# Moving the fourth step size from chunk 1 to chunk 4 and re-spreading the layer-norm squares in a selective-scan kernel

## The chip, the cores and the metric

The kernel runs on one core of a Trainium2 chip. The metric is the device time of one execution in microseconds (us), median of three runs. The core has five engines with a program each: TensorE (PE, matmuls), VectorE (DVE), ScalarE (ACT), GpSimd (POOL) and SyncE (SP, which issues the DMAs). They are ordered against each other by semaphores alone: each engine runs its own list in order, and a waiting instruction holds up all behind it.

## The reference, cut to what matters

Input x is 16 batches of 1024 steps by 512 channels. Two layers follow, each on a layer norm of x and added to x:

```
xn = layernorm(x)                               # layer norm 1
xp = xn @ x_proj_w.T                            # 64 + 16 + 16 columns: d_rank, B, C
delta = softplus(d_rank @ dt_proj_w.T + dt_b)   # the step size, 512 channels
h[t] = exp(delta * A) * h[t-1] + delta * B * xn # 16 states per channel
y[t] = sum over the states of h[t] * C + xn * D
x = x + y
weights = layernorm(x) @ router_w + router_b    # layer norm 2
...                                             # the 127 highest rows of each batch go through
                                                # attention and an MLP; the others take layernorm(x)
```

The change lies in the first layer's phase, the scan phase; the router's weights are its last product.

## The kernel before, in words

The scan phase (`scan_phase`) takes the 16 batches one after the other. A batch has 16 chunks of 32 channels. A chunk has 4 groups, each of 4 states x 32 channels = 128 partitions, and a group's tile is 128x1024, all 1024 steps. So a batch has 64 tiles. (c,g) is group g of chunk c. Batch 0 and batch 15 are written out, the others run in a loop over pairs of batches.

For each tile: ACT makes `decay` = exp(A * delta) into one of two PSUM buffers (L600); DVE makes `inp` = dx * B (L722), in chunks 1 and 3 to 13 POOL does it for group 3 (L844, the table `OWN_AT`); DVE scans, `hid` (L733); POOL multiplies by C, `ch` (L879); PE sums the states into `ps_y` (`sum_states`, L399). After a chunk ACT copies the sum (`copy_y`, L615), PE turns it (`turn_y`, L408), and DVE adds it to x (`add_y`, L743). The addition for chunk c stands in DVE's list behind the third scan of chunk c+1, so it needs `ch` (c,3) by then. `hid`, `ch` and `inp` have four buffers each, one per group. ACT's list per chunk: `decay` for groups 2 and 3, `copy_y`, `copy_dx` (L608), `decay` for groups 0 and 1 of the next chunk; `beside` puts other work between them at four places, 0 ahead of group 2's decay, 1 behind `copy_dx`, 2 and 3 behind the two decays. At the top of the file tables say at which (chunk, place) on ACT, or (chunk, group) on PE and POOL, that other work stands:

- The step size of a block of 128 channels (k = 0 to 3, each used by four chunks): PE makes two halves of z into the one bank `aux` (`step_size`, L382), ACT reads each half twice (`z_half`, L509 and L510) and then runs four passes (`exp_log`, L517 to L524), and POOL makes four more steps (`delta`, L853, L856, L860, L865), placed by the table `DELTA`. Blocks 0 to 2 are made for the next batch in chunks 12, 13 and 15 (`Z`); block 3 for the current batch, in chunk `Z3`. Chunks 12 to 15 are its users.
- Layer norm 1 of the next batch (`SUMS1`) and layer norm 2 of the batch before (`SUMS2`): 17 steps each, 0 to 7 sums (L541), 8 the mean (L544), 9 to 16 squares (L547), then `rstd`, three small operations. POOL finishes them (`newton`, L805 to L828) at `FINISH1` = (7,0) and `FINISH2` = (2,1).
- `copy_rw` (L528) puts the router's weights into `aux` at (2,0); DVE's `router` (L755) reads it behind the scans of chunks 2 and 3.
- The rows of the next batch are normalised by ACT (L470), turned by PE into `aux` (`turn_xhat`, L365) and copied (L483) in chunks 7 to 10, and projected in chunks 10 and 11.

`aux` is one PSUM bank; its users take turns by `aux_emptied` and `aux_full`, and the router's use of it is guarded by `router_sum`.

Of the kernel before, what the change touches and what calls it, by code (L numbers as in the profile page):

```python
# [26 lines left out]
TC = L // P  # L27
# [9 lines left out]
PROJECT = (((10, 0), (10, 0), (10, 1), (10, 1)), ((10, 3), (11, 0), (11, 0), (11, 1)))  # L37
COPY_PROJ = ((10, 3), (11, 3))

SUMS1 = {(5, 1): range(0, 2), (5, 2): range(2, 4), (5, 3): range(4, 8), (6, 0): range(8, 10), (6, 1): range(10, 12), (6, 2): range(12, 14), (6, 3): range(14, 17)}  # L40
SUMS2 = {(0, 1): range(0, 2), (0, 2): range(2, 4), (0, 3): range(4, 8), (1, 0): range(8, 10), (1, 1): range(10, 12), (1, 2): range(12, 14), (1, 3): range(14, 17)}
MAKE_OUT = ((3, 1), (3, 1), (3, 2), (3, 2), (3, 3), (3, 3), (3, 3), (3, 3))
NORM1 = 7


Z = (12, 13, 15)
Z3 = 1


DELTA = {(13, 0): (1, 0, 0), (13, 1): (1, 0, 1), (13, 2): (1, 0, 2), (13, 3): (1, 0, 3),  # L50
# [3 lines left out]

RW_COPY = (2, 0)
ROUTER = (2, 3)
# [10 lines left out]
USE = {key: u for u, key in enumerate(USES)}  # L67
NUSE = len(USES)
# [8 lines left out]
def xhat_slot(k, par):  # L77

    return (0, k) if k < 2 else (1 + par, k - 2)


def scan_phase(nc, semaphores, x, A_log, w_xproj, w_dt, dt_b, D_col, router_w, router_b, ident_c, nsum_c, bc_dram,
               x1_dram, w_dram, out, nb_run=B):

    with ExitStack() as ctx:
# [83 lines left out]
        aux_emptied = sem("aux_emptied")  # L169
# [13 lines left out]
        router_sum = sem("router_sum")  # L183
# [18 lines left out]
        def has(b, least):  # L202

            return not isinstance(b, int) or b >= least
# [145 lines left out]
        @block.tensor  # L350
        def _(pe):
            def aux_free(b, key):

                u = USE[key]
                if has(b, 1) or u > 0:
                    pe.wait_ge(aux_emptied, b * NUSE + u)

            def turn_xhat(b, t):

                aux_free(b, ("xhat", t))  # L360
                if t == 0 and has(b, 2):
                    pe.wait_ge(router_sum, b * TC - TC)
                pe.wait_ge(xh_ready, b * TC + t + 1)
                for k in range(KD):
                    last = pe.transpose(aux[:, k * P:(k + 1) * P], xh[:, t % 2, k * P:(k + 1) * P], ident[:])  # L365
                last.then_inc(aux_full, 1)

            def project(b, par, h, ks=range(KD)):

                if 0 in ks:  # L370
                    aux_free(b, ("proj", h))
                for k in ks:
                    last = pe.matmul(aux[0:R + 2 * N, :], xproj[:, k, :],
                                     xhT[:, xhat_slot(k, par)[0], xhat_slot(k, par)[1], h * HALF:(h + 1) * HALF],
                                     start=(k == 0), stop=(k == KD - 1))
                if KD - 1 in ks:
                    last.then_inc(aux_full, 1)

            def step_size(b, k, h):

                aux_free(b, ("z", k, h))
                pe.matmul(aux[:], dtw[:, k * P:(k + 1) * P], xpT[0:R, h * HALF:(h + 1) * HALF],  # L382
                          start=True, stop=True).then_inc(aux_full, 1)

            def sum_states(b, par, c, g):

                if g == 0 and (has(b, 1) or c > 0):

                    pe.wait_ge(y_added, b * CHUNKS + c)
                k = c // NT  # L390
                if g == 0:
                    i, j = xhat_slot(k, par)
                    for q in range(4):
                        pe.matmul(ps_y[q * CH:(q + 1) * CH, 0:2 * P],  # L394
                                  dskip[:, k, c % NT * CH:(c % NT + 1) * CH],
                                  xhT[:, i, j, q * 2 * P:(q + 1) * 2 * P], start=True, stop=False)
                pe.wait_ge(ch_ready, tile(b, c, g) + 1)
                for q in range(4):
                    last = pe.matmul(ps_y[q * CH:(q + 1) * CH, 0:2 * P], nsum[:],  # L399
                                     ch[:, g, q * 2 * P:(q + 1) * 2 * P],  # L400
                                     start=False, stop=(g == GROUPS - 1))
                last.then_inc(ch_summed, 1)

            def turn_y(b, c):

                pe.wait_ge(ysb_ready, b * CHUNKS + c + 1)
                for t in range(2):
                    last = pe.transpose(ps_y[:, (2 + t) * P:(3 + t) * P], ysb[:, t * P:(t + 1) * P], ident[:])  # L408
                last.then_inc(yt_ready, 1)

            pe.wait_ge(consts_in, 16 * NCONST)
            for t in range(TC):
                turn_xhat(0, t)
            for h in range(2):
                project(0, 0, h)
            for k in range(3):
                for h in range(2):
                    step_size(0, k, h)
            pe.wait_ge(dskip_ready, KD)

            def body(b, par):
                final = is_last(b)
                for c in range(CHUNKS):
                    if c > 0:
                        turn_y(b, c - 1)
                    elif has(b, 1):
                        turn_y(b - 1, CHUNKS - 1)
                    for g in range(GROUPS):
                        sum_states(b, par, c, g)

                        for h, at in ((0, (-1, 3)), (1, (0, 0))):
                            if (c, g) == (Z3 + at[0], at[1]):
                                step_size(b, 3, h)
                            for k in range(3):
                                if (c, g) == (Z[k] + at[0], at[1]) and not final:
                                    step_size(b + 1, k, h)
                        if final:
                            continue
                        for t in range(TC):
                            if TURN[t] == (c, g):  # L440
                                turn_xhat(b + 1, t)
                        for h in range(2):
                            for k in range(KD):
                                if PROJECT[h][k] == (c, g):
                                    project(b + 1, 1 - par, h, (k,))

            batches(pe, body)
            turn_y(nb_run - 1, CHUNKS - 1)

            pe.wait_ge(wcol_ready, nb_run)  # L450
            pe.wait_ge(aux_emptied, nb_run * NUSE)
            pe.transpose(aux[0:nb_run * TC, 0:P], wcol[:, 0:nb_run * TC], ident[:]).then_inc(wt_ready, 1)
# [3 lines left out]
        def _(act):  # L456
# [66 lines left out]
                act.wait_ge(z_act, n + 4)  # L523
                nc.scalar.activation(tu[:], tu[:], ACT.Identity, scale=-1.0, bias=1.0).then_inc(z_act, 1)  # L524

            def copy_rw(b):

                nc.scalar.activation(aux[:], rw[:], ACT.Copy).then_inc(rw_ready, 1)  # L528

            def sums(b, par, steps, norm, m, chain_act):  # L530
# [114 lines left out]
            def beside(b, par, c, place):  # L645

                at = (c, place)
                if c == Z3 and place == 1:
                    z_half(b, 3, 0)
                if c == Z3 and place == 3:  # L650
                    z_half(b, 3, 1)
                    exp_log(b, 3)
                if has(b, 1):
                    if at == RW_COPY:
                        copy_rw(b - 1)
                    if at in SUMS2:
                        ln2_sums(b - 1, 1 - par, SUMS2[at])
                    for t in range(TC):
                        if MAKE_OUT[t] == at:
                            make_out(b - 1, 1 - par, t)  # L660
                if is_last(b):
                    return
                if at in SUMS1:
                    ln1_sums(b + 1, 1 - par, SUMS1[at])
                if at == (NORM1, 2):
                    for t in range(2):
                        normalise(b + 1, 1 - par, t)
                for t in range(TC):
                    if COPY_XHAT[t] == at:
                        copy_xhat(b + 1, 1 - par, t)  # L670
                        if t + 2 < TC:
                            normalise(b + 1, 1 - par, t + 2)
                for h in range(2):
                    if COPY_PROJ[h] == at:
                        copy_proj(b + 1, h)
                if c in Z and place == 1:
                    z_half(b + 1, Z.index(c), 0)
                if c in Z and place == 3:
                    z_half(b + 1, Z.index(c), 1)
                    exp_log(b + 1, Z.index(c))  # L680
# [20 lines left out]
            batches(act, body)  # L701
            last = nb_run - 1
            copy_y(last, CHUNKS - 1)
            copy_rw(last)
            ln2_sums(last, 1, range(17))
            for t in range(TC):
                make_out(last, 1, t)
# [1017 lines left out]
```

## Time and profile before

| | us |
|---|---|
| median of 3 runs | 4733.67 (4727.59 to 4733.85) |
| profiled execution | 4730.44 |
| its span | 4728.3 |
| DVE busy | 3868.9 (82%) |
| POOL busy | 3543.6 (75%) |
| PE busy | 2806.7 (59%) |
| ACT busy | 2752.0 (58%) |

The scan phase takes the first 3640 us or so of the span, the second layer the rest. In the scan phase a pattern of some 222 us repeats, one batch. The tables in which the page groups instructions add up all batches; to see where an engine waits within a batch one reads the timeline of one of them. Idle time of an engine costs something only where another one is waiting for what it makes next. Rows below are mostly of batch 7, a batch from the middle.

### The profile page before, as it was taken

The numbers are of one execution on the slowest core, as the hardware profiler recorded it, in microseconds if no ns is written. First come the engines' busy times: TensorE is split into PE (matmuls) and PEld (weight loads), VectorE is DVE, ScalarE is ACT, GpSimd is POOL, SyncE is SP. The second block draws the span as 40 slices with busy tenths as digits, with TensorE's granted clock in tenths as the row PEclk, the third lists the DMA queues.
The fourth block names the chain that finished last, engine by engine and source line by source line (L and its number), as shares of the span: only waits on it lengthen the run. The fifth ranks groups of instructions, "written<-read, shape, count | busy, mean of one in ns | idle before, by whom it ended". The sixth has DMA issues, their size and how long they took to land. (4 is left out here: it accounts for less than half of the span.)

```text
span 4728.3 us, 57323 instructions
## 1 busy us (share of the span) xinstructions
PE 2806.7 (59%) x15590; PEld 1068.8 (23%) x15590; DVE 3868.9 (82%) x3306; ACT 2752.0 (58%) x4103; POOL 3543.6 (75%) x1796
## 2 busy tenths in 40 slices
PE   3555464546464645555454546464642399999997
PEld 1111111111121111111111111111110255555553
DVE  3999999999999999999999999999997644444442
ACT  5676766766767667676766766767754222222221
POOL 4999999999999999999999999999995100000000
PEclk7556565656565656556565656565655599999998
DMA  4454545364544545454545364545533200000000
GB/s 101 96 130 116 142 104 154 85 160 100 147 114 129 131 112 133 111 130 116 141 105 155 82 160 100 146 112 133 135 93 114 82 14 18 18 18 18 18 18 7
DMA packets 198209, 472.73 MB, mean 100 GB/s; under 512 B 60688, under 2 KB 61200, under 8 KB 197088
## 3 DMA queue, kind: packets, MB, share of 16 engines
q1 hardware_dynamic: 177136, 452.11, 37.8%
q0 software_dynamic: 20736, 16.88, 1.3%
q8 instruction: 120, 1.97, 0.2%
q14 instruction: 217, 1.78, 0.1%
HBM read 126.83 MB, written 73.43 MB: 42 GB/s over the span
## 5 line engine op out<-in xcount | busy, mean ns | idle before, releaser
L879 POOL TENSOR_TENSOR ch<-hid,cmat 128x1024 f32<-128x1024 f32 x1024 | 2387.2, 2354 | 101.0 <-DVE hid L733 84.1
L733 DVE TENSOR_TENSOR_SCAN hid<-decay,inp 128x1024 f32<-128x1024 f32 x1024 | 2289.2, 2274 | 96.3 <-ACT decay L600 94.2
L600 ACT ACTIVATE decay<-delr,a_neg 128x1024 f32<-128x1024 f32 x1024 | 1136.7, 1112 | 811.8 <-DVE hid L733 801.0
L399 PE MATMUL ps_y<-ch,nsum 128*32 128x256 f32 x8192 | 1000.3, 588 | 854.9 <-POOL ch L879 850.9
L722 DVE TENSOR_TENSOR inp<-dx,bmat 128x1024 f32<-128x1024 f32 x832 | 959.3, 1211 | 63.2 <-ACT dx L608 63.2
L399 PEld LDWEIGHTS ps_y<-ch,nsum 128*32 128x32 f32 x8192 | 249.0, 143 | 1591.5 <-POOL ch L879 1364.2
L408 PE MATMUL ps_y<-ident,ysb 128*128 128x128 f32 x512 | 168.9, 431 | 683.3 <-ACT ysb L615 666.7
L844 POOL TENSOR_TENSOR inp<-dxr,bmat 128x1024 f32<-128x1024 f32 x192 | 452.4, 2356 | 0.0
L1133 POOL DMA_INDIRECT out_rows<-row,idx_out x16 | 41.1, 2570 | 458.9 <-issue 252.4
L394 PE MATMUL ps_y<-xhT,dskip 128*32 128x256 f32 x2048 | 271.9, 623 | 142.5 <-DVE xr L743 142.5
L408 PEld LDWEIGHTS ps_y<-ident,ysb 128*128 128x128 f32 x512 | 71.3, 196 | 909.4 <-ACT ysb L615 865.9
L608 ACT ACTIVATE dx<-dxr 128x1024 f32<-128x1024 f32 x256 | 260.8, 1019 | 3.0 <-DMA dxr<-dxT 3.0
L382 PE MATMUL aux<-xpT,dtw 64*128 64x512 f32 x256 | 238.9, 1030 | 21.2 <-ACT dxT L510 20.5
L1195 PE MATMUL ps_t<-w,h2T 128*128 128x512 f32 x512 | 226.1, 600 | 11.9 <-ACT h2T L1334 11.9
L1219 PE MATMUL ps_m<-w,gT 128*128 128x512 f32 x512 | 224.9, 592 | 0.0
L1099 POOL COPY idx_x<-cols_i 128x1 uint32 (+1 forms) x16 | 4.7, 297 | 252.8 <-DMA out_rows<-row,idx_out 175.4
L547 ACT ACTIVATE squares<-xr,m 128x512 bf16<-128x512 f32 x256 | 181.7, 713 | 1.0
L853 POOL TENSOR_TENSOR tu<-tu,te 128x1024 f32<-128x1024 f32 x64 | 150.8, 2356 | 36.4 <-ACT tu L524 36.4
L1573 DVE TENSOR_SCALAR GT<-ps_t 128x512 f32<-128x512 f32 x32 | 22.0, 691 | 185.7 <-PE ps_t L1190 185.7
L743 DVE TENSOR_TENSOR xr<-xr,ps_y 128x256 f32<-128x256 f32 x256 | 106.3, 415 | 76.0 <-PE ps_y L408 68.3
L541 ACT ACTIVATE squares<-xr 128x512 bf16<-128x512 f32 x256 | 157.4, 617 | 14.3 <-DVE xr L743 14.2
L1099 POOL COPY idx_m<-cols_i 128x1 uint32 (+1 forms) x16 | 2.9, 180 | 207.3 <-PE ps_t L1190 204.7
(167 smaller groups left out, 3921.7 us busy)
## 6 DMA issues: line engine op xcount, KB each, us to landing
dxr<-dxT SPq DMA_DIRECT2D x1024, 128.0 KB, 2.4
delr<-delT SPq DMA_DIRECT2D x1024, 128.0 KB, 2.4
xr<-in_x SPq DMA_DIRECT2D x32, 1024.0 KB, 5.5
bmat<-b_and_c SPq DMA_DIRECT2D x256, 128.0 KB, 3.4
cmat<-b_and_c SPq DMA_DIRECT2D x256, 128.0 KB, 2.9
x_rows<-xr SPq DMA_DIRECT2D x16, 2048.0 KB, 7.6
out_rows<-xr SPq DMA_DIRECT2D x32, 1024.0 KB, 4.3
w<-in_w SPq DMA_DIRECT2D x2, 4096.0 KB, 23.7
```

The lines of the kernel that those rows point to most:

```text
L382: pe.matmul(aux[:], dtw[:, k * P:(k + 1) * P], xpT[0:R, h * HALF:(h + 1) * HALF], start=True, stop=True).then_inc(aux_full, 1)
L394: pe.matmul(ps_y[q * CH:(q + 1) * CH, 0:2 * P], dskip[:, k, c % NT * CH:(c % NT + 1) * CH], xhT[:, i, j, q * 2 * P:(q + 1) * 2 * P], start ...
L399: last = pe.matmul(ps_y[q * CH:(q + 1) * CH, 0:2 * P], nsum[:], ch[:, g, q * 2 * P:(q + 1) * 2 * P], start=False, stop=(g == GROUPS - 1))
L408: last = pe.transpose(ps_y[:, (2 + t) * P:(3 + t) * P], ysb[:, t * P:(t + 1) * P], ident[:])
L600: nc.scalar.activation(decay[:, g % 2, :], delr[:, c % 2, :], ACT.Exp, scale=a_neg[:, i:i + 1])\
L608: nc.scalar.activation(dx[:], dxr[:, c % 2, :], ACT.Copy).then_inc(dx_ready, 1)
L722: nc.vector.tensor_tensor(inp[:, g, :], dx[:], bmat[:, g, :], ALU.mult).then_inc(inp_ready, 1)
L733: nc.vector.tensor_tensor_scan(hid[:, g, :], decay[:, g % 2, :], inp[:, g, :], 0.0, ALU.mult, ALU.add).then_inc(hid_ready, 1)
L844: nc.gpsimd.tensor_tensor(inp[:, OWN, :], dxr[:, c % 2, :], bmat[:, OWN, :], ALU.mult)\
L879: nc.gpsimd.tensor_tensor(ch[:, g, :], hid[:, g, :], cmat[:, g, :], ALU.mult).then_inc(ch_ready, 1)
L1195: last = pe.matmul(one[bank], xT[:, k, :], w(k), start=(k == 0), stop=(k == n - 1))
L1219: last = pe.matmul(one["m1"], gT[:, k, :], w_2[:, k, :], start=(k == 0), stop=(k == F // P - 1))
```

## The change

Four tables, two placements and two waits are changed; no instruction is added or taken away, and the second layer is untouched.

- `Z3` goes from 1 to 4. ACT's two halves of z for block 3 and the four passes stand in chunk 4. PE makes the first half behind group 3 of chunk 3 (before: chunk 0) and the second behind group 1 of chunk 4 (before: behind group 0 of chunk 1).
- POOL's four steps for block 3 go from (3,2), (4,0), (4,2), (5,0) to (5,2), (6,0), (6,2), (7,1).
- The steps of layer norm 2 go from chunks 0 to 1 to places from (0,2) to (2,0), those of layer norm 1 start at (5,2) instead of (5,1); both are spread more evenly.
- `copy_rw` stands behind the last squares at (2,0) and waits for the bank to be empty after block 2's z; PE's wait for the router goes from the first `turn_xhat` to block 3's first `step_size`.

```diff
--- before.py
+++ after.py
@@ -37,20 +37,20 @@
 PROJECT = (((10, 0), (10, 0), (10, 1), (10, 1)), ((10, 3), (11, 0), (11, 0), (11, 1)))
 COPY_PROJ = ((10, 3), (11, 3))
 
-SUMS1 = {(5, 1): range(0, 2), (5, 2): range(2, 4), (5, 3): range(4, 8), (6, 0): range(8, 10), (6, 1): range(10, 12), (6, 2): range(12, 14), (6, 3): range(14, 17)}
-SUMS2 = {(0, 1): range(0, 2), (0, 2): range(2, 4), (0, 3): range(4, 8), (1, 0): range(8, 10), (1, 1): range(10, 12), (1, 2): range(12, 14), (1, 3): range(14, 17)}
+SUMS1 = {(5, 2): range(0, 2), (5, 3): range(2, 5), (6, 0): range(5, 8), (6, 1): range(8, 11), (6, 2): range(11, 14), (6, 3): range(14, 17)}
+SUMS2 = {(0, 2): range(0, 3), (0, 3): range(3, 6), (1, 0): range(6, 8), (1, 1): range(8, 11), (1, 2): range(11, 13), (1, 3): range(13, 15), (2, 0): range(15, 17)}
 MAKE_OUT = ((3, 1), (3, 1), (3, 2), (3, 2), (3, 3), (3, 3), (3, 3), (3, 3))
 NORM1 = 7
 
 
 Z = (12, 13, 15)
-Z3 = 1
+Z3 = 4
 
 
 DELTA = {(13, 0): (1, 0, 0), (13, 1): (1, 0, 1), (13, 2): (1, 0, 2), (13, 3): (1, 0, 3),
          (14, 1): (1, 1, 0), (14, 3): (1, 1, 1), (15, 2): (1, 1, 2), (1, 0): (0, 1, 3),
          (0, 2): (0, 2, 0), (1, 2): (0, 2, 1), (2, 0): (0, 2, 2), (3, 0): (0, 2, 3),
-         (3, 2): (0, 3, 0), (4, 0): (0, 3, 1), (4, 2): (0, 3, 2), (5, 0): (0, 3, 3)}
+         (5, 2): (0, 3, 0), (6, 0): (0, 3, 1), (6, 2): (0, 3, 2), (7, 1): (0, 3, 3)}
 
 RW_COPY = (2, 0)
 ROUTER = (2, 3)
@@ -358,8 +358,6 @@
             def turn_xhat(b, t):
 
                 aux_free(b, ("xhat", t))
-                if t == 0 and has(b, 2):
-                    pe.wait_ge(router_sum, b * TC - TC)
                 pe.wait_ge(xh_ready, b * TC + t + 1)
                 for k in range(KD):
                     last = pe.transpose(aux[:, k * P:(k + 1) * P], xh[:, t % 2, k * P:(k + 1) * P], ident[:])
@@ -379,6 +377,8 @@
             def step_size(b, k, h):
 
                 aux_free(b, ("z", k, h))
+                if k == 3 and h == 0 and has(b, 1):
+                    pe.wait_ge(router_sum, b * TC)
                 pe.matmul(aux[:], dtw[:, k * P:(k + 1) * P], xpT[0:R, h * HALF:(h + 1) * HALF],
                           start=True, stop=True).then_inc(aux_full, 1)
 
@@ -428,9 +428,10 @@
                     for g in range(GROUPS):
                         sum_states(b, par, c, g)
 
+                        for h, at in ((0, (Z3 - 1, 3)), (1, (Z3, 1))):
+                            if (c, g) == at:
+                                step_size(b, 3, h)
                         for h, at in ((0, (-1, 3)), (1, (0, 0))):
-                            if (c, g) == (Z3 + at[0], at[1]):
-                                step_size(b, 3, h)
                             for k in range(3):
                                 if (c, g) == (Z[k] + at[0], at[1]) and not final:
                                     step_size(b + 1, k, h)
@@ -523,8 +524,9 @@
                 act.wait_ge(z_act, n + 4)
                 nc.scalar.activation(tu[:], tu[:], ACT.Identity, scale=-1.0, bias=1.0).then_inc(z_act, 1)
 
-            def copy_rw(b):
-
+            def copy_rw(b, emptied):
+
+                act.wait_ge(aux_emptied, emptied)
                 nc.scalar.activation(aux[:], rw[:], ACT.Copy).then_inc(rw_ready, 1)
 
             def sums(b, par, steps, norm, m, chain_act):
@@ -651,10 +653,10 @@
                     z_half(b, 3, 1)
                     exp_log(b, 3)
                 if has(b, 1):
-                    if at == RW_COPY:
-                        copy_rw(b - 1)
                     if at in SUMS2:
                         ln2_sums(b - 1, 1 - par, SUMS2[at])
+                    if at == RW_COPY:
+                        copy_rw(b - 1, b * NUSE + USE["z", 2, 1] + 1)
                     for t in range(TC):
                         if MAKE_OUT[t] == at:
                             make_out(b - 1, 1 - par, t)
@@ -701,7 +703,7 @@
             batches(act, body)
             last = nb_run - 1
             copy_y(last, CHUNKS - 1)
-            copy_rw(last)
+            copy_rw(last, nb_run * NUSE)
             ln2_sums(last, 1, range(17))
             for t in range(TC):
                 make_out(last, 1, t)
```

ACT's list in the last batch, chunk 1 into chunk 2, before; from block 3's second half of z to the decays (2,2) and (2,3):
```order
L509 ACTIVATE te<-aux,dtb 128x512
L510 ACTIVATE dxT<-aux,dtb 128x512
L517 ACTIVATE te<-te 128x1024
L521 ACTIVATE tu<-te 128x1024
L522 ACTIVATE delT<-te 128x1024
L524 ACTIVATE tu<-tu 128x1024
L547 ACTIVATE squares,m<-xr,m 128x512 x3
L576 ACTIVATE r<-m,eps 128x8
L579 ACTIVATE r<-r 128x8
L581 ACTIVATE r<-r 128x8
L528 ACTIVATE aux<-rw 128x512
L600 ACTIVATE decay<-delr,a_neg 128x1024 x2
```
The same place now, from chunk 1's copy of dx:
```order
L610 ACTIVATE dx<-dxr 128x1024
L546 ACTIVATE m<-m 128x8
L549 ACTIVATE squares,m<-xr,m 128x512 x2
L602 ACTIVATE decay<-delr,a_neg 128x1024
L549 ACTIVATE squares,m<-xr,m 128x512 x2
L602 ACTIVATE decay<-delr,a_neg 128x1024
L549 ACTIVATE squares,m<-xr,m 128x512 x4
L578 ACTIVATE r<-m,eps 128x8
L581 ACTIVATE r<-r 128x8
L583 ACTIVATE r<-r 128x8
L530 ACTIVATE aux<-rw 128x512
L602 ACTIVATE decay<-delr,a_neg 128x1024 x2
```
The z work is gone, and the mean and the squares that stood ahead of the copy of dx are here now; eight squares instead of seven.

PE's list in batch 0, chunks 0 and 1, before:
```order
L394 MATMUL ps_y<-xhT,dskip 32x256 x4
L399 MATMUL ps_y<-ch,nsum 32x256 x16
L382 MATMUL aux<-xpT,dtw 128x512
L408 MATMUL ps_y<-ident,ysb 128x128 x2
L394 MATMUL ps_y<-xhT,dskip 32x256 x4
L399 MATMUL ps_y<-ch,nsum 32x256 x4
L382 MATMUL aux<-xpT,dtw 128x512
```
And chunks 3 and 4 now:
```order
L394 MATMUL ps_y<-xhT,dskip 32x256 x4
L399 MATMUL ps_y<-ch,nsum 32x256 x16
L382 MATMUL aux<-xpT,dtw 128x512
L408 MATMUL ps_y<-ident,ysb 128x128 x2
L394 MATMUL ps_y<-xhT,dskip 32x256 x4
L399 MATMUL ps_y<-ch,nsum 32x256 x8
L382 MATMUL aux<-xpT,dtw 128x512
L399 MATMUL ps_y<-ch,nsum 32x256 x8
```
Both products of L382 have moved three chunks, and the second stands behind eight matmuls of L399 (two groups) instead of four (one).

POOL's list in batch 0, chunks 3 and 4, before (a chunk ends with the own input, L844):
```order
L865 TENSOR_TENSOR dxT<-delT,xhT 128x1024
L879 TENSOR_TENSOR ch<-hid,cmat 128x1024 x2
L853 TENSOR_TENSOR tu<-tu,te 128x1024
L879 TENSOR_TENSOR ch<-hid,cmat 128x1024
L844 TENSOR_TENSOR inp<-dxr,bmat 128x1024
L879 TENSOR_TENSOR ch<-hid,cmat 128x1024
L856 TENSOR_TENSOR delT<-delT,tu 128x1024
L879 TENSOR_TENSOR ch<-hid,cmat 128x1024 x2
L860 TENSOR_TENSOR delT<-delT,dxT 128x1024
L879 TENSOR_TENSOR ch<-hid,cmat 128x1024
L844 TENSOR_TENSOR inp<-dxr,bmat 128x1024
L879 TENSOR_TENSOR ch<-hid,cmat 128x1024
```
The end of chunk 5 and chunk 6 now (line numbers are two higher):
```order
L855 TENSOR_TENSOR tu<-tu,te 128x1024
L881 TENSOR_TENSOR ch<-hid,cmat 128x1024
L846 TENSOR_TENSOR inp<-dxr,bmat 128x1024
L881 TENSOR_TENSOR ch<-hid,cmat 128x1024
L858 TENSOR_TENSOR delT<-delT,tu 128x1024
L881 TENSOR_TENSOR ch<-hid,cmat 128x1024 x2
L862 TENSOR_TENSOR delT<-delT,dxT 128x1024
L881 TENSOR_TENSOR ch<-hid,cmat 128x1024
L846 TENSOR_TENSOR inp<-dxr,bmat 128x1024
L881 TENSOR_TENSOR ch<-hid,cmat 128x1024
```
Steps of block 3 (L853, L856, L860 before) stood in chunks 3 and 4, which held seven 128x1024 operations each; now chunk 6 is the one with seven, and the last step (L867) follows in chunk 7 behind the small operations of layer norm 1.

## Rows read from the trace of the kernel before

**Rows 1.** The page, part 1: each engine's busy us, share of the span, instructions.
```profile
PE 2806.7 (59%) x15590; PEld 1068.8 (23%) x15590; DVE 3868.9 (82%) x3306; ACT 2752.0 (58%) x4103; POOL 3543.6 (75%) x1796
```

**Rows 2.** Windows, batch 7: length, busy us (x instructions), clock, DMA.
```profile
1632.17:1854.49 222.32, 117.92 (x736) 34.67 (x736) 211.25 (x149) 155.15 (x228) 215.23 (x107) 0.58 0.50 125
```

**Rows 3.** Waits, 300 to 3600 us: who waited for whom, total us, times, longest.
```profile
DVE hid L733 <- ACT decay L600: 88.3, 33, 5.9
...
ACT xhT L483 <- PE aux L365: 59.4, 42, 1.9
...
DVE xr L743 <- PE ps_y L408: 56.4, 64, 1.5
```

**Rows 4.** Timeline, DVE, scan (2,2): start, us, what [idle before <-releaser].
```profile
1666.48 2.29 DVE L733 TENSOR_TENSOR_SCAN hid<-decay,inp 128x1024 f32<-128x1024 f32 x1 [4.83 <-ACT decay L600]
```

**Rows 5.** Timeline, ACT, chunk 1 into 2 of batch 7.
```profile
1650.10 0.68 ACT L509 ACTIVATE te<-aux,dtb 128x512 f32<-128x512 f32 x1
...
1651.24 0.72 ACT L547 ACTIVATE squares<-xr,m 128x512 bf16<-128x512 f32 x1
...
1656.14 0.68 ACT L509 ACTIVATE te<-aux,dtb 128x512 f32<-128x512 f32 x1
...
1661.74 0.71 ACT L547 ACTIVATE squares<-xr,m 128x512 bf16<-128x512 f32 x1
...
1665.19 2.14 ACT L600 ACTIVATE decay<-delr,a_neg 128x1024 f32<-128x1024 f32 x2
```

**Rows 6.** Lines by form, batch 7: squares and sums; busy us, mean ns.
```profile
L547 ACT ACTIVATE squares<-xr,m 128x512 bf16<-128x512 f32 x16 | 11.4, 714 | 0.1
...
L541 ACT ACTIVATE squares<-xr 128x512 bf16<-128x512 f32 x16 | 9.8, 616 | 1.6 <-DVE xr L743 1.6
```

**Rows 7.** Timeline, POOL, chunks 3 to 12 of batch 7.
```profile
1679.98 2.34 POOL L879 TENSOR_TENSOR ch<-hid,cmat 128x1024 f32<-128x1024 f32 x1 [3.44 <-DVE hid L733]
...
1707.69 0.19 POOL L833 TENSOR_TENSOR r<-r 128x8 f32<-128x8 f32 x1
...
1708.31 2.34 POOL L879 TENSOR_TENSOR ch<-hid,cmat 128x1024 f32<-128x1024 f32 x1
...
1717.55 6.97 POOL L879 TENSOR_TENSOR ch<-hid,cmat 128x1024 f32<-128x1024 f32 x3
...
1740.59 0.24 POOL L805 TENSOR_TENSOR r<-r 128x8 f32<-128x8 f32 x1
...
1742.03 6.98 POOL L879 TENSOR_TENSOR ch<-hid,cmat 128x1024 f32<-128x1024 f32 x3
...
1797.97 9.39 POOL L879 TENSOR_TENSOR ch<-hid,cmat 128x1024 f32<-128x1024 f32 x4 [0.42 <-DVE hid L733]
```

**Rows 8.** Timeline, DVE, chunks 4 to 6 of batch 7.
```profile
1700.30 2.28 DVE L733 TENSOR_TENSOR_SCAN hid<-decay,inp 128x1024 f32<-128x1024 f32 x1
...
1705.88 6.64 DVE L733 TENSOR_TENSOR_SCAN hid<-decay,inp 128x1024 f32<-128x1024 f32 x3
1713.10 0.42 DVE L743 TENSOR_TENSOR xr<-xr,ps_y 128x256 f32<-128x256 f32 x1 [0.58 <-PE ps_y L408]
1713.43 2.28 DVE L733 TENSOR_TENSOR_SCAN hid<-decay,inp 128x1024 f32<-128x1024 f32 x1
...
1726.96 0.42 DVE L743 TENSOR_TENSOR xr<-xr,ps_y 128x256 f32<-128x256 f32 x1 [1.31 <-PE ps_y L408]
```

**Rows 9.** Timeline, PE, ACT and DVE, chunk 12 into 13 of batch 7.
```profile
1806.64 2.79 PE L399 MATMUL ps_y<-ch,nsum 128*32 128x256 f32 x24
...
1806.75 0.69 ACT L509 ACTIVATE te<-aux,dtb 128x512 f32<-128x512 f32 x1 [0.68 <-PE aux L382]
...
1811.85 2.14 ACT L600 ACTIVATE decay<-delr,a_neg 128x1024 f32<-128x1024 f32 x2
...
1813.14 2.29 DVE L733 TENSOR_TENSOR_SCAN hid<-decay,inp 128x1024 f32<-128x1024 f32 x1 [0.46 <-ACT decay L600]
```

**Rows 10.** Timeline, ACT, `decay` (7,2) of batch 7.
```profile
1735.19 1.12 ACT L600 ACTIVATE decay<-delr,a_neg 128x1024 f32<-128x1024 f32 x1 [0.24 <-DVE hid L733]
```

## The prediction

> **What bounds the kernel now.** I read the page first (part 1, engine totals, [rows 1]), then busy time over one batch of the scan phase, then the waits of VectorE (DVE) and GpSimd (POOL), and last the timeline of one batch, number 7, engine by engine. In the page DVE is the busiest engine, 82% against 75% for POOL [rows 1]. Over batch 7 alone, 222.32 us from its first `ch` to the next batch's, POOL is busy 215.23 us and DVE 211.25 us [rows 2]. So both are nearly full, and POOL is the fuller one. What is left to gain in a batch is their idle time: about 7 us on POOL, 11 us on DVE. (c,g) below is group g of chunk c.
>
> DVE's waits in the scan phase are of two kinds [rows 3]: 88.3 us, 33 times, for ScalarE's (ACT) `decay`, 56.4 us for PE's turned y. The largest of the first is once a batch at scan (2,2): 4.83 us in batch 7, so that DVE could have scanned at 1661.65 [rows 4]. Of the 33, fifteen are these, fifteen are 0.46 us at (13,2) [rows 9], and three others are under 1 us each; so the wait at (2,2) is (88.3 - 6.9 - 2.4) / 15 = 5.3 us on average. ACT's rows say why [rows 5]: in chunk 1 it makes the fourth step size (1650.10, and from 1656.14 to 1661.74), with passes of layer norm 2 around it, and comes to `decay` (2,2) at 1665.19. POOL then starves too: 3.44 us before `ch` (3,0) [rows 7]. The second kind is POOL's lateness in disguise: DVE's y addition in chunk c waits for `ch` (c-1,3). In chunk 4 that `ch` starts 5.73 us after its scan ends (1708.31 against 1700.30 + 2.28), and the next addition waits 0.58; in chunk 5 it is 6.45 us (third of the three from 1717.55, against 1713.43 + 2.28), and the next waits 1.31 [rows 7, 8]. So the wait is the lag less 5.15 us. That line is what I use for the new places.
>
> **The change part by part.** Durations are of the profiled execution, whose own time is 4730.44 us (span 4728.3 us and 2.1 around it); the median of the runs is 4733.67, 3.2 above. Instruction counts stay the same; everything is a matter of place.
>
> *ACT in chunks 0 to 2.* The z work that goes from ACT ahead of (2,2) is 1.14 us (1650.10 to 1651.24) and 5.60 (1656.14 to 1661.74): 6.74 us [rows 5]. The sums are pushed later: behind the copy of dx in chunk 1 stood seven squares, now eight and the small mean. A square's pitch is 0.70 us, a first-pass sum's 0.62 (means 0.714 and 0.616 less what neighbours overlap [rows 6]); so 0.96 is added. `decay` (2,2) could start at 1665.19 - 6.74 + 0.96 = 1659.4; to delay nothing it must start by 1661.65 less its 1.1, 1660.5. The whole wait at (2,2) goes, with 1.1 us to spare. Ahead of that, chunks 0 and 1 hold eight sums (5.0 us) in idle ACT time: nothing. `copy_rw` now waits for a slot emptied a chunk earlier: nothing.
>
> *POOL behind it.* `ch` (3,0) moves up by the 3.44 us of starvation, no more, since then POOL itself is behind: the gain of 5.3 is not all usable.
>
> *POOL in chunks 3 to 7.* A slot (one 128x1024 operation) is 2.315 us, from (6.98 - 2.35)/2, three in 6.98 us with 2.35 for one (the row at 1742.03, [rows 7]). A chunk has four `ch`, mostly one own input, and the delta steps. Before, chunks 3 to 7 hold 7, 7, 6, 5, 5 slots; now 6, 5, 6, 7, 6: the sum is the same, the place is later, and chunk 7 has in addition the five small ln1 operations, 1.44 us (1740.59 to 1742.03). A DVE chunk without gaps is 12.55 us (from the addition at 1713.10 to that at 1726.96, less 1.31 [rows 8]), or 5.4 slots. Walking batch 7:
> - `ch` (3,0) at 1676.5; eleven slots and 0.6 us of routing (1707.69 to 1708.31) later POOL could begin (5,0) at 1702.6. DVE's scan (5,0) ends at 1705.88 + 2.28 - 4.83 = 1703.3. POOL is idle 0.7 us again.
> - Scan (5,2), a new wait. Chunk 12 shows the same z work in a chunk of 12.55: the second half starts at 1806.75, after 0.68 us of waiting for PE's step product; `decay` comes at 1811.85 and DVE waits 0.46 [rows 9]. In chunk 4 PE's second product stands one sum of states further back (after group 1 instead of group 0); a sum's pitch is 0.86 us: three sums (x24) take 2.79 us, one alone 1.08, and (2.79 - 1.08)/2 = 0.86 [rows 9]. So DVE waits 0.46 + 0.86 = 1.3 us at (5,2), scan (5,2) ends at 1709.0 instead of 1707.7, and POOL, ready at 1707.9, idles 1.1.
> - From 1709.0 POOL needs 9 slots to `ch` (6,3), 1729.9. DVE's scan (6,3) ends at 1724.1. Lag 5.8, so the addition in chunk 7 waits 0.65.
> - POOL needs 6 slots and 1.44 to `ch` (7,3), 1745.2; scan (7,3) ends at 1724.1 + 12.55 + 0.65 = 1737.3. Lag 7.9, the addition in chunk 8 waits 2.75.
> - Chunks 8 to 11 have 5 slots (11.6 us) against 12.55: the lag falls by 1 us each and is gone at (12,0), where POOL has waited 0.42 until now [rows 7]. It does not reach chunk 13 with its eight slots.
>
> DVE in batch 7: -4.83 - 0.58 - 1.31 + 1.3 + 0.65 + 2.75 = -2.0 us. POOL's side must agree: -3.44 + 0.7 + 1.1 - 0.42 = -2.1. It does. With the average wait of 5.3 in place of 4.83 DVE comes to -2.5 (POOL then idles 0.25 at (5,0) instead of 0.7).
>
> *ACT in chunks 5 to 7.* The first-pass sums of layer norm 1 start a place later, and 0.96 us more (a mean and a square) stands between the copy of dx in chunk 6 and `decay` (7,2). That one started at 1735.19 after 0.24 us of idling [rows 10], so it will be 0.96 - 0.24 = 0.7 late. A `decay` (1.12) has one scan (2.28, pitch 2.19) to hide in, so it may be 1.05 late for free: nothing here, at most 0.2. The wait on `router_sum` moves from the transposes of chunk 7 to the step product behind group 3 of chunk 3. On PE only the turning of y 3 is behind it, due a chunk's half later: nothing, but if that cover were gone each us would hit DVE's addition.
>
> *The sum.* 14 batches at -2.5, -35; the last batch has no ln1 operations in chunk 7, so only 2.75 - 1.44 at (8,3), -3.8; the first is POOL-bound throughout and gains nothing to 0.5. Total -39 us: 4691.5 for the profiled execution, 4695 on the median.
>
> Between bounds: the wait at (5,2) is 0.46 at the least (as in chunk 12) and 2.3 at the most (two more sums). At the least, POOL idles 0.3 instead of 1.1 and gives back 0.8 a batch, 12 us: -51 in all. At the most it idles 1.0 more: -24.
>
> **The rivals.**
> *The whole wait is won.* If DVE is the bound and POOL's lag is only cosmetic, the change gives 15 x 5.3 = 79 us less the 15 x 1.3 at (5,2): -60, 4674; at the extreme -79, 4655. For it: DVE is the busiest engine of the page [rows 1], and its additions wait only 0.6 and 1.3 us now. Against it: POOL's 215.23 of 222.32 us [rows 2]; a batch can't be under that plus what POOL must idle. The Trainium skill (Perfetto Trace Analysis, Identifying the Most-Contended Engine) says to take the engine of highest occupancy and close its gaps; by the page's totals that is DVE and this rival's time, by the batch's totals it is POOL and mine. Chance 0.15.
>
> *The gain is eaten in chunks 5 to 8.* Step size and deltas cost in their new place what they cost in the old: a wait of 2.3 at (5,2), and over 4 at (8,3) since normalising in chunk 7 waits for POOL's late ln1 operations. For it: the same work in the same 12.55 us chunk, and ACT's waits for PE there. Against: chunk 12 does it for 0.46. Time about 4728, within 0.2% (the least that a measurement tells from no change, 9.5 us). Chance 0.08.
>
> *Slower.* The mechanism is the eight transposes of the normalised rows (chunks 7 to 9): each stands on PE behind a sum of states, so behind POOL's `ch`, and ACT stands still for its copy with the decays queued behind; 42 such waits cost up to 1.9 us now [rows 3] and nothing on DVE. With POOL's lag at 6.5 instead of 3.1 us at (8,0), each of the three copies in chunks 7 and 8 could be 3.4 later. A `decay` may be 1.05 late for free, so three times 2.3 is 7 us a batch; less the 2.5 gained, +4.5, over 15 batches +68: 4801. It decides only if ACT's wait passes the slack of the first two decays of a chunk, 3.5 us and more; I find it passing only once, by 0.1 to 0.2, where the 2.75 at (8,3) hides it. Chance 0.05.
>
> **How the numbers follow.** The forecast, POOL-bound with a gain of 24 to 51 us, has 0.65; the whole wait 0.15; the same 0.08; slower 0.05; and 0.07 lies between forecast and no change. Time 4695. For 8 in 10 the range goes from 4671 (just into the first rival) to 4715. Faster 0.87, same 0.08, slower 0.05.
>
> **What would show it.** In the new profile: no wait of DVE at (2,2) and no 3.44 us on POOL at (3,0); a wait for `decay` of about 1.3 us at (5,2); the waits for turned y gone from (5,3) and (6,3) and standing at (7,3), some 0.65, and (8,3), some 2.75; POOL idle about 1 us at (5,2), none at (12,0); a batch some 2.5 us shorter than now, 219.5 to 220. Wrong if the additions in chunks 7 and 8 don't wait, if the batch is under 218, or if decays wait in chunks 7 to 9.

## The result, and the profile after

The changed kernel takes 4691.51 us (median of 4 runs, 4689.1 to 4692.74), the kernel before 4731.57 us beside it; the ratio is 0.9912, 95% interval 0.9899 to 0.9924. That is 40 us less, against 39 forecast; the time forecast on the median was 4695. DVE's wait for `decay` (2,2), its waits at the additions of chunks 5 and 6 and POOL's starvation at (3,0) are gone. Smaller waits of DVE at (5,2), in chunks 7 and 8 and in chunk 2 are new.

Batch 7 over its own windows, from its first `ch` to the next batch's (columns as in [rows 2]: length, busy us of PE, PE loads, DVE, ACT, POOL, clock, DMA):

```profile
1618.48:1838.39 219.91, 115.77 (x736) 34.85 (x736) 211.37 (x149) 155.03 (x228) 215.34 (x107) 0.57 0.50 126
```

The work is the same to 0.1 us on DVE and POOL; the batch is 2.4 us shorter, and POOL is now idle 4.6 us of it instead of 7.1. Over all batches the waits between 300 and 3600 us, the view of [rows 3]:

```profile
DVE xr L745 <- PE ps_y L408: 81.2, 76, 4.1
ACT xhT L484 <- PE aux L363: 70.3, 42, 2.0
...
DVE hid L735 <- ACT decay L602: 24.6, 36, 1.3
...
DVE hid L735 <- POOL ch L881: 7.0, 16, 0.9
```

The wait for decays fell by 63.7 us (88.3 to 24.6), and the wait for the turned y rose by 24.8 (56.4 to 81.2). But the view of before ends ahead of the last addition of the phase, which stands at 3624.53 there and at 3587.47 now, with a wait of 4.1 us in both. The whole phase, from 0 to 3700 us, is the fairer view; before:

```profile
DVE hid L733 <- ACT decay L600: 94.2, 36, 5.9
DVE xr L743 <- PE ps_y L408: 68.3, 70, 4.1
...
DVE hid L733 <- POOL ch L879: 1.9, 2, 1.0
```

and now:

```profile
DVE xr L745 <- PE ps_y L408: 87.1, 81, 4.1
...
DVE hid L735 <- ACT decay L602: 31.6, 39, 4.4
...
DVE hid L735 <- POOL ch L881: 7.4, 17, 0.9
```

That is -62.6, +18.8 and +5.5, together -38.3 us, and the last addition stands 37.1 us earlier.

ACT at (2,2), the place of [rows 5], and DVE there, the place of [rows 4]:

```profile
1644.77 0.58 ACT L530 ACTIVATE aux<-rw 128x512 f32<-128x512 f32 x1
1645.38 1.12 ACT L602 ACTIVATE decay<-delr,a_neg 128x1024 f32<-128x1024 f32 x1
```

```profile
1643.07 6.64 DVE L735 TENSOR_TENSOR_SCAN hid<-decay,inp 128x1024 f32<-128x1024 f32 x3
```

The three scans (2,0), (2,1), (2,2) run on without a break; `decay` (2,2) starts as soon as scan (2,0) has ended, which was also when ACT came to it.

POOL in chunks 3 to 8, the stretch of [rows 7]:

```profile
1662.32 2.35 POOL L881 TENSOR_TENSOR ch<-hid,cmat 128x1024 f32<-128x1024 f32 x1
...
1676.71 6.96 POOL L881 TENSOR_TENSOR ch<-hid,cmat 128x1024 f32<-128x1024 f32 x3 [0.47 <-DVE hid L735]
...
1689.32 4.65 POOL L881 TENSOR_TENSOR ch<-hid,cmat 128x1024 f32<-128x1024 f32 x2 [0.40 <-DVE hid L735]
1695.11 2.37 POOL L881 TENSOR_TENSOR ch<-hid,cmat 128x1024 f32<-128x1024 f32 x1 [1.13 <-DVE hid L735]
...
1728.87 4.66 POOL L881 TENSOR_TENSOR ch<-hid,cmat 128x1024 f32<-128x1024 f32 x2
```

`ch` (3,0) at 1662.32 follows its own input at once: the 3.44 us are gone. At (4,0) and (5,0) POOL idles 0.47 and 0.40, at (5,2) 1.13. DVE over the same chunks (scan (5,2), the additions that stand in chunks 6 and 7, scan (7,3), scan (8,2) and the addition that stands in chunk 8; compare [rows 8]):

```profile
1692.74 2.29 DVE L735 TENSOR_TENSOR_SCAN hid<-decay,inp 128x1024 f32<-128x1024 f32 x1 [1.32 <-ACT decay L602]
...
1707.53 0.42 DVE L745 TENSOR_TENSOR xr<-xr,ps_y 128x256 f32<-128x256 f32 x1
...
1720.71 0.42 DVE L745 TENSOR_TENSOR xr<-xr,ps_y 128x256 f32<-128x256 f32 x1 [0.63 <-PE ps_y L408]
1721.05 2.28 DVE L735 TENSOR_TENSOR_SCAN hid<-decay,inp 128x1024 f32<-128x1024 f32 x1
...
1731.32 2.29 DVE L735 TENSOR_TENSOR_SCAN hid<-decay,inp 128x1024 f32<-128x1024 f32 x1 [0.23 <-POOL ch L881]
1735.97 0.42 DVE L745 TENSOR_TENSOR xr<-xr,ps_y 128x256 f32<-128x256 f32 x1 [2.37 <-PE ps_y L408]
```

1.32 at (5,2), 0.63 at (7,3), and in chunk 8 0.23 + 2.37 = 2.60. `ch` (7,3) starts at 1731.18 (second of the two from 1728.87), 7.85 us after its scan's end at 1723.33: the lag that the last wait follows from.

### The profile page after: what moved, and what is told of

The parts are those of the page before. It is cut to its first block and busy times, and to the rows that moved or that the text cites. A ratio compares the mean times of both kernels' runs of the same rounds, so it can differ in the third digit from the quotient of the medians.

```text
span 4690.7 us, 57331 instructions
## 1 busy us (share of the span) xinstructions
PE 2815.9 (60%) x15590; PEld 1085.7 (23%) x15590; DVE 3870.3 (83%) x3306; ACT 2754.4 (59%) x4103; POOL 3546.0 (76%) x1796
## 5 line engine op out<-in xcount | busy, mean ns | idle before, releaser
L399 PE MATMUL ps_y<-ch,nsum 128*32 128x256 f32 x8192 | 1001.4, 594 | 903.2 <-POOL ch L881 900.6
L399 PEld LDWEIGHTS ps_y<-ch,nsum 128*32 128x32 f32 x8192 | 260.1, 146 | 1617.7 <-POOL ch L881 1369.0
L382 PE MATMUL aux<-xpT,dtw 64*128 64x512 f32 x256 | 237.6, 1025 | 21.2 <-ACT dxT L511 20.5
L371 PE MATMUL aux<-xhT,xproj 128*96 128x512 f32 x256 | 160.5, 751 | 1.4 <-ACT xhT L484 0.7
```

## The experiments

All are compared with the kernel before on the same chip. Its medians beside them are 4732.09 and 4732.45 us, against 4731.57 beside the changed kernel, so medians of different experiments are compared with each other below. Averages per batch are over batches 1 to 15 of the profiled execution. Diffs are against the changed kernel, where nothing else is said.

### PE's second product one group earlier

```diff
-                        for h, at in ((0, (Z3 - 1, 3)), (1, (Z3, 1))):
+                        for h, at in ((0, (Z3 - 1, 3)), (1, (Z3, 0))):
```

> The changed kernel, with PE's second step product of block 3 behind group 0 of chunk 4 instead of group 1. Theory (POOL-bound, and the wait at (5,2) is PE's place in the queue): the wait at (5,2) falls by one sum of states, 0.86 us, to 0.46, in the batches where it is 1.32 now; POOL idles 0.3 instead of 1.1 us there; a batch is 0.5 to 0.86 shorter, the kernel 8 to 12 us: about 4681. Rival (the lag of POOL takes it back at (7,3) and (8,3)): the wait at (5,2) falls but those two grow by as much, and the time stays at 4691.

Measured: 4680.93 us, ratio 0.9897 [0.9881, 0.9914]. Between 300 and 3600 us:

```profile
DVE xr L745 <- PE ps_y L408: 77.7, 72, 4.3
POOL ch L881 <- DVE hid L735: 31.3, 52, 4.3
DVE hid L735 <- ACT decay L602: 17.1, 35, 0.8
```

No wait for a decay is longer than 0.8 us now, and their sum fell by 7.5; the wait for the turned y did not grow (81.2 to 77.7), against the rival. The wait at (5,2) is 0.46 or 0.47 us in each of batches 1 to 14 (0.37 in batch 15), where it was 0.97 on average, and POOL's idle time there fell from 0.79 to 0.27. So PE's place in its queue was the cause of the part that went, and POOL's idle time there was real cost. Fifteen times 0.51 us is 7.7; the medians differ by 10.6 us. The intervals of the two ratios overlap, so the size is known less well than the wait.

### The old tables for the layer norms, the new place for the step size

```diff
-SUMS1 = {(5, 2): range(0, 2), (5, 3): range(2, 5), (6, 0): range(5, 8), (6, 1): range(8, 11), ...
-SUMS2 = {(0, 2): range(0, 3), (0, 3): range(3, 6), (1, 0): range(6, 8), (1, 1): range(8, 11), ...
+SUMS1 = {(5, 1): range(0, 2), (5, 2): range(2, 4), (5, 3): range(4, 8), (6, 0): range(8, 10), ...
+SUMS2 = {(0, 1): range(0, 2), (0, 2): range(2, 4), (0, 3): range(4, 8), (1, 0): range(8, 10), ...
```

> The changed kernel with the old tables for the steps of both layer norms; block 3's step size stays in chunk 4. Theory (the gain is the move of the z work out of chunk 1; the spreading is worth nothing by itself): 4689 to 4695, no wait at (2,2). Rival (the spreading is needed, since chunk 1 with its squares is still crowded): a wait of 1 us or more at (2,2), 4700 or more.

Measured: 4688.33 us, ratio 0.9909 [0.9892, 0.9926], not to be told from the change as a whole, and with no wait at (2,2). No gain of the spreading of the squares can be seen once the z work is out of chunk 1.

### The new tables for the layer norms alone

Against the kernel before:

```diff
-SUMS1 = {(5, 1): range(0, 2), ...      # both tables as in the change
+SUMS1 = {(5, 2): range(0, 2), ...
-                    if at == RW_COPY:
-                        copy_rw(b - 1)
                     if at in SUMS2:
                         ln2_sums(b - 1, 1 - par, SUMS2[at])
+                    if at == RW_COPY:
+                        copy_rw(b - 1)
```

> The kernel before with only the new tables for the steps of both layer norms (copy_rw behind the squares at (2,0)); block 3's step size stays in chunk 1. Theory: one square and the mean more, 0.96 us, stand ahead of decay (2,2), so its wait grows from 5.3 to some 6.2 us and POOL starves as much longer at (3,0): 15 times 0.9, about 13 us slower than the kernel before, 4745. Rival (spreading the sums is a gain of its own): 4720 or less.

Measured: 4743.57 us, ratio 1.0025 [1.0015, 1.0035], 11.5 us slower than before. The waits, beside the 88.3 us of [rows 3]:

```profile
DVE hid L733 <- ACT decay L600: 101.6, 37, 6.9
```

13.3 us more, near the 15 x 0.9 us expected of the 0.96 us of ACT work that the tables put behind the copy of dx in chunk 1. At (2,2) itself the wait grew by 0.82 us on average (5.28 to 6.10). POOL's starvation at (3,0) grew by less than expected, from 3.43 to 3.95 us. With the experiment before, the change is split: the move of the step size is the whole gain, as far as the times can tell, and the tables alone are a loss.

### One slot of POOL's given to DVE

```diff
-OWN_AT = (1, 3, 4, 5, 6, 7, 8, 9, 10, 11, 12, 13)
+OWN_AT = (1, 3, 4, 5, 6, 8, 9, 10, 11, 12, 13)
```

> The changed kernel with the input of (7,3) made by DVE instead of POOL: DVE has one operation more a batch (1.15 us), POOL one slot less (2.3 us). Theory (POOL sets the pace in chunks 5 to 8): the lag at (7,3) falls from 7.9 to about 4.5 us, the wait at (8,3) goes (and the one before it at (8,2)), the one at (7,3) shrinks since DVE has four inputs in chunk 6; a batch is 1.5 to 2.1 us shorter, 22 to 32 in all: 4660 to 4670. Rival (DVE, the busiest engine of the page, is the bound, and waits of 0.6 and 2 us come from elsewhere, as PE or ACT): 15 times 1.15, 17 us slower: 4708.

Measured: 4655.75 us, ratio 0.984 [0.9824, 0.9857]: DVE has 1.15 us more to do in each batch, and the kernel is 36 us faster than the changed one. DVE from the inputs of chunk 7 to chunk 8 in batch 7 (four inputs at 1695.19 in place of three, and no bracket with a wait behind them):

```profile
1695.19 4.59 DVE L724 TENSOR_TENSOR inp<-dx,bmat 128x1024 f32<-128x1024 f32 x4
...
1706.39 0.42 DVE L745 TENSOR_TENSOR xr<-xr,ps_y 128x256 f32<-128x256 f32 x1
...
1719.01 0.42 DVE L745 TENSOR_TENSOR xr<-xr,ps_y 128x256 f32<-128x256 f32 x1
1719.34 2.28 DVE L735 TENSOR_TENSOR_SCAN hid<-decay,inp 128x1024 f32<-128x1024 f32 x1
```

The additions in chunks 7 and 8 (1706.39 and 1719.01) don't wait, 12.62 us apart; the lag at (7,3) is 4.9 us on average, under the 5.15 at which a wait begins. So the waits of 0.63 and 2.60 us were POOL's load and nothing of PE or ACT. The gain is a little over the 22 to 32 us expected. The wait at (7,3) went wholly: 0.63 + 2.60 - 1.15 = 2.1 us a batch, 33 us over 16. Another 3 us are no work of the edit: the wait at (5,2) was 0.79 us on average in this run, against 0.97.

### POOL's steps spread over chunks 5 to 8

```diff
-         (5, 2): (0, 3, 0), (6, 0): (0, 3, 1), (6, 2): (0, 3, 2), (7, 1): (0, 3, 3)}
+         (5, 2): (0, 3, 0), (6, 2): (0, 3, 1), (7, 3): (0, 3, 2), (8, 2): (0, 3, 3)}
```

> The changed kernel with POOL's last three steps of block 3 later: (6,2), (7,3), (8,2) instead of (6,0), (6,2), (7,1), so that chunks 5 to 8 hold six slots each instead of 6, 7, 6, 5. Theory (POOL's total work and what it must idle set the pace, not the crowding of single chunks): the waits at (7,3) and (8,3) go, but POOL is no less busy, and one wait of about 2.4 us comes at (9,3); what can be gained is POOL's idle time at (13,0), 0.8 us a batch: 0 to 12 us, 4680 to 4691. Rival (the crowding of chunks 6 and 7 is what costs): the 3.1 us of waits at (7,3), (8,2) and (8,3) go for good, 45 us, 4646.

Measured: 4677.44 us, ratio 0.9886 [0.9871, 0.9901], 14 us less than the changed kernel (the intervals touch), where 0 to 12 were expected. DVE in batch 7, scan (8,3) and the addition that stands in chunk 9:

```profile
1725.30 2.29 DVE L735 TENSOR_TENSOR_SCAN hid<-decay,inp 128x1024 f32<-128x1024 f32 x1 [0.41 <-POOL inp L846]
...
1739.27 0.42 DVE L745 TENSOR_TENSOR xr<-xr,ps_y 128x256 f32<-128x256 f32 x1 [1.74 <-PE ps_y L408]
```

The waits at (7,3) and in chunk 8 went, and in their place came, on average, 0.4 us at scan (8,3), which waits for POOL's input, and 1.7 at the addition in chunk 9. POOL no longer idles at (13,0), where it had idled 0.79. That is the 0.8 us a batch that could be had, 12 us, and not the 45 us of the rival: even load on POOL moves the wait, less load removes it.

### Both edits together

```diff
-OWN_AT = (1, 3, 4, 5, 6, 7, 8, 9, 10, 11, 12, 13)
+OWN_AT = (1, 3, 4, 5, 6, 8, 9, 10, 11, 12, 13)
-                        for h, at in ((0, (Z3 - 1, 3)), (1, (Z3, 1))):
+                        for h, at in ((0, (Z3 - 1, 3)), (1, (Z3, 0))):
```

> The changed kernel with both edits that made it faster: PE's second step product behind group 0 of chunk 4, and the input of (7,3) made by DVE. Theory (DVE is the bound from chunk 5 on once POOL has a slot less, so the wait at (5,2) counts in full on DVE): 4656 less 15 times 0.5, about 4647. Rival (the two save the same idle time of POOL): no faster than 4656.

Measured: 4650.19 us, ratio 0.9827 [0.9813, 0.984], 5.6 us less than with POOL's slot alone; 8 were expected. With POOL's slot alone the wait at (5,2) was 0.79 us on average, and it is 0.45 here: 15 x 0.34 = 5.1 us, close to what the times say. Against the rival, then, the second edit still wins something, but the intervals overlap, so this is likely and not shown by the times. Together the two bring 41 us, less than the 10.6 and 35.8 us of each alone.

### PE's product ahead of the turning of y 14

```diff
-                                if (c, g) == (Z[k] + at[0], at[1]) and not final:
+                                if (c, g) == (Z[k] + at[0], at[1] - (k == 2 and h == 0)) and not final:
```

on top of both edits.

> As the kernel with both edits, and PE's first step product of block 2 of the next batch behind group 2 of chunk 14 instead of group 3, so that it does not stand ahead of the turning of y 14. Theory (from chunk 13 to chunk 4 POOL, with 8, 6, 5, 6, 6, 6 slots, sets the pace, and the 1.5 us wait at (15,3) is its lag as much as PE's queue): the wait at (15,3) shrinks to 0.2, but as much comes back at (2,3); within 3 us of the kernel with both edits. Rival (that wait is PE's queue alone): 15 times 1.3, 20 us faster, about 4627.

Measured: 4647.76 us, ratio 0.9821 [0.9807, 0.9834], the same as with both edits. The wait at (15,3) fell from 1.4 to 0.8 us on average, and those at (0,3) and (2,3) grew from 0.2 each to 0.5 and 0.7: given back within three chunks. The wait at (15,3) fell less than the expected 1.3 us. What holds the rest was not tested; POOL's lag at (14,3) is 6.0 us with and without the edit.

### A second slot given to DVE

```diff
-OWN_AT = (1, 3, 4, 5, 6, 8, 9, 10, 11, 12, 13)
+OWN_AT = (3, 4, 5, 6, 8, 9, 10, 11, 12, 13)
```

on top of that.

> As the kernel with the third block's product moved, and the input of (1,3) made by DVE too (1.15 us more a batch on DVE, a slot of 2.3 us less on POOL, at the end of chunk 0). Theory: POOL's lag from chunk 13 is now worked off by chunk 1, the wait at (2,3) goes, and DVE keeps the 1.3 us of (15,3): 1.3 + 0.4 - 1.15 = 0.5 us a batch better than the kernel with both edits, about 8 us, 4639. Rival (DVE is the bound already, and every operation put on it costs its time): 17 us slower than that kernel, about 4664.

Measured: 4656.49 us, ratio 0.984 [0.9827, 0.9853], 8.7 us slower than the kernel before this edit. This expectation failed. The kernel without the edit, and with it:

```profile
DVE xr L745 <- PE ps_y L408: 39.2, 49, 4.8
POOL ch L881 <- DVE hid L735: 36.8, 57, 4.3
```

```profile
POOL ch L881 <- DVE hid L735: 76.6, 80, 4.4
DVE xr L745 <- PE ps_y L408: 25.5, 37, 4.4
```

DVE's wait for the turned y fell by 13.7 us, its work grew by 15 x 1.15 = 17.3, and POOL starves 39.8 us more. These two terms of DVE make +3.6 us, and the profiled executions differ by 3.5; the medians differ by 8.7, and the rest isn't explained. I had counted the 1.3 us of (15,3) as still to be won, though only 0.6 of it had gone and that was already in the kernel compared with; the wait there is 0.8 us in both. With this edit DVE has no wait over 0.2 us in chunks 1 to 4, and POOL idles 1.14 us at (1,0) and 1.73 at (4,0) where it had idled 0 and 0.22: DVE is the bound there, and only the 0.7 us wait at (2,3) could be won for 1.15 us of work. The rival's sign was right, its size (17 us) was not.

## Why the prediction was right

- *The wait at (2,2) goes whole.* So it did. The z work was forecast to let `decay` (2,2) start with 1.1 us to spare; ACT came to it at 1645.38, and scan (2,2) began some 2 us later (the third of the three from 1643.07, 2.19 apart), so 1.0 us was to spare beyond its own 1.1. The sums do cost something there when the z work stays: the experiment with the tables shows 0.82 us at (2,2).
- *POOL sets what can be used of it.* Of 5.3 us a batch on DVE 2.4 stayed (219.52 us a batch on average after, 221.89 before, over batches 1 to 14; 2.5 forecast). The first batch gained nothing and the last 3.8 us, as forecast. The experiment that gives DVE an operation more and gets faster settles it: a bound on DVE would have made that 17 us slower.
- *The wait at (5,2), 1.3 us.* 1.32 in eight of the batches, among them batch 7, with POOL idle 1.13 (1.1 forecast). In the other seven it was 0.2 to 0.9 (see below), which the forecast did not have: 1.0 on average. The sum of states that stands more ahead of PE's product was tested as the cause by moving the product back.
- *(7,3) 0.65 and chunk 8 2.75.* Measured 0.63 and 2.60. The line "wait = lag less 5.15" carried to the new places; 7.85 - 5.15 = 2.70. A part, 0.23 in batch 7 and up to 0.6 in even batches, came not at the addition but at scan (8,2), which waited for its `hid` buffer: a kind that I had not listed, and that takes from the other, so the sum stood.
- *POOL idle at (5,0) 0.7, none at (12,0).* Measured 0.47 at (4,0) and 0.40 at (5,0) in batch 7, together 0.87, and nothing before `ch` (12,0). Batch 7 is one of two with so much at (4,0); on average the two places have 0.5 us, where the forecast had 0.25. At (13,0), which the lag was not to reach, POOL idles 0.79 instead of 0.90.
- *What was missed.* The addition in chunk 2 now waits 0.5 us on average, a term that the forecast did not have. It stands right behind scan (2,2), and before, that scan's wait of 5.3 us covered it: the lag at (1,3) was 6.4 us already. It is 2.15 us in batch 3 and 2.01 in batch 11, and under 0.8 in the others. POOL in batch 3:

```profile
747.95 2.36 POOL L881 TENSOR_TENSOR ch<-hid,cmat 128x1024 f32<-128x1024 f32 x1 [3.64 <-DMA cmat<-b_and_c]
```

In batch 3 POOL had waited 3.64 us at (0,2) for the DMA of C and stayed late until chunk 2. POOL's idle time at (0,2) rose from 0.57 us on average to 0.83, some 4 us in the profiled run. It varies from run to run of like kernels and was not studied. The smaller wait at (5,2) gave back some 5 us (15 x 0.33). The two about cancel, so the closeness of the sum, 40 against 39, is partly luck; its terms were each right to some 0.5 us a batch. The profiled executions, 4730.44 and 4692.74 us, differ by 37.7.
- *A miscount.* Of the 33 waits for decays in [rows 3], fourteen and not fifteen are those at (13,2), and four and not three are others, at (0,2). The average of 5.3 us at (2,2) stays.
- *The rivals.* All three are out. Against the gain being eaten, scan (5,2) and chunk 8 wait 1.3 and 2.6 us in batch 7, not 2.3 and over 4. The slower one's mechanism is visible, ACT's waits for the transposes rose from 59.4 to 70.3 us [rows 3], but no decay of chunks 7 to 9 came late.

## What to carry to other kernels

Where two engines are each some 96% busy, walk both through the pattern and keep their lag as a number: removing a wait on one wins at most the idle time that the other had with it, and a lag that is too long shows up as a wait for some third engine (here PE). The rule that converts lag to wait can be read off two places of the old trace and used at new ones that have the same work between: in chunk 2 DVE makes four inputs and not three, 1.13 us more, so the bound there is 6.28 in place of 5.15, and the new lag of 6.72 at (1,3) fits its wait of 0.5. It does not hold at (15,3): a lag of 6.0 us goes with a wait of 1.5 there, since PE has the product of block 2 ahead of the turning of y 14, as the experiment with that product shows in part. A long wait can cover such a lag just behind it. When two engines can do the same operation, moving one from the engine that lags to the one that waits can pay where the lag peaks: the first such move, at the peak, brought 36 us, the second, where little lag was left to win, cost 9. Other places weren't tried. The fastest versions (both edits, with or without the third) take 4650.19 and 4647.76 us, 82 and 85 us under the 4732.45 us of the kernel before beside them.

## What the runs showed of the hardware

The wait at (5,2) varied with TensorE's clock. In batch 7 PE's second product (two matmuls) took 2.07 us at a granted clock of 0.50 (1.2 GHz), in batch 5 the same product 1.12 us at 1.00 (2.4 GHz):

```profile
1684.24 2.07 PE L382 MATMUL aux<-xpT,dtw 64*128 64x512 f32 x2
```

```profile
1247.02 1.12 PE L382 MATMUL aux<-xpT,dtw 64*128 64x512 f32 x2
```

```profile
1247.02:1248.14 1.12, 1.12 (x10) 0.36 (x10) 1.12 (x2) 0.75 (x1) 1.09 (x2) 1.00 1.02 397
1684.24:1686.31 2.07, 2.07 (x10) 0.57 (x10) 2.07 (x3) 0.58 (x1) 2.07 (x2) 0.50 1.04 399
```

(length, then busy us of PE, PE loads, DVE, ACT, POOL, then the granted clock and the DMA's share and GB/s.) DVE in batch 5 waits

```profile
1254.57 2.29 DVE L735 TENSOR_TENSOR_SCAN hid<-decay,inp 128x1024 f32<-128x1024 f32 x1 [0.21 <-ACT decay L602]
```

0.21 instead of 1.32 us. The other batches fit: the product took 2.07 us in all eight batches that waited 1.32, and 1.12 to 1.69 us, at a mean granted clock of 0.65 to 1.00, in the seven that waited 0.21 to 0.93. Ahead of both products shown PE had done the same: it turned y and then ran matmuls back to back from the D term on, 2.6 us in batch 5 and 2.7 in batch 7. So what raises the clock in some batches and not in others is open. With the product one group earlier (the first experiment) 1.9 us of matmuls stand back to back ahead of it, and in all 16 batches it took 2.07 us at 0.50. A wait that ends at one matmul on a short path can differ by a microsecond from batch to batch with the clock alone, and one batch of a trace does not show it.
